# Attention round: the convolution's bias as a two-row product on TensorE, and statistics read from the PSUM bank

## The reference, cut to what matters

```
xp = einsum('mn,bnf->bmf', L_norm, x)
h  = xp @ Wc + bc                      # bc: a row of 128, the same for every node
h  = relu(layernorm(h) * g1 + be1)
x1 = h + x                             # q, k, v, attention, projection, two more layer norms follow
```

## Time and profile before

| | us |
|---|---|
| median of 3 runs | 1043.13 |
| lowest and highest | 1039.88, 1051.63 |
| the profiled execution's own time | 1042.99 |
| its span, first to last instruction | 1041.2 |
| VectorE busy in the span | 638.5 |
| TensorE busy in the span | 938.3 |
| TensorE's granted clock, mean | 0.946 |

### The profile page before, as it was taken

One profiled execution on the slowest core, in us unless ns is written; L12 is line 12 of the kernel. 1 busy time (PEld: TensorE's weight loads), 2 busy tenths in 40 slices (PEclk: granted clock), 3 DMA queues, 4 the chain that ended last, 5 costly groups with the idle time before them and its releaser, 6 DMA issues. The chain is left out here.

```text
span 1041.2 us, 21243 instructions
## 1 busy us (share of the span) xinstructions
PE 938.3 (90%) x7030; PEld 750.0 (72%) x7030; DVE 638.5 (61%) x2077; ACT 519.5 (50%) x1127; POOL 323.8 (31%) x405
## 2 busy tenths in 40 slices
PE   5998899999999999895999999999899999879771
PEld 4556799999999999875777767767676776647451
DVE  4743233333333335344788878878788888746998
ACT  2232322322332222212888877878787887855430
POOL 0000111111111112122335544545454553236665
PEclk8887999999999999898999998999999999989995
DMA  3000000000000000004544444544343444300111
GB/s 89 1 1 10 11 11 10 10 10 10 10 10 10 20 10 11 1 1 122 123 123 123 122 122 121 121 117 115 98 116 93 117 116 120 83 1 21 41 50 50
DMA packets 47199, 61.19 MB, mean 59 GB/s; under 512 B 4377, under 2 KB 22050, under 8 KB 47138
## 3 DMA queue, kind: packets, MB, share of 16 engines
q1 hardware_dynamic: 47138, 60.51, 22.7%
HBM read 39.53 MB, written 20.97 MB: 58 GB/s over the span
## 5 line engine op out<-in xcount | busy, mean ns | idle before, releaser
L1534 ACT ACTIVATE prob<-prob,low 128x512 f32<-128x512 f32 x256 | 184.1, 719 | 63.3 <-DVE low L1584 61.4
L1584 DVE CUSTOM_DVE_ANT_0 prob<-bank,mask 128x512 f32<-128x512 f32 x256 | 172.5, 685 | 41.5 <-PE bank L1413 24.7
L1426 PE MATMUL bank<-ident,prob 128*128 128x128 f32 x1024 | 164.7, 284 | 11.1 <-ACT probT L1523 11.0
L1426 PEld LDWEIGHTS bank<-ident,prob 128*128 128x128 f32 x1024 | 115.9, 143 | 58.4 <-issue 34.0
L1413 PE MATMUL bank<-k_stack,q_stack 128*128 128x512 f32 x256 | 125.4, 491 | 16.5 <-DVE low L1584 11.6
L1523 ACT ACTIVATE probT<-bank 128x512 f32<-128x512 f32 x176 | 102.5, 582 | 3.0 <-PE bank L1426 1.1
L1059 DVE TENSOR_TENSOR T_lo<-bank,T_hi 128x512 fp32r<-128x512 f32 x48 | 33.0, 688 | 112.0 <-ACT T_hi L897 112.0
L897 ACT ACTIVATE T_hi<-bank 128x512 fp32r<-128x512 f32 x48 | 28.4, 592 | 134.6 <-PE bank L807 91.6
L595 POOL TENSOR_SCALAR var_eps<-mv 128x4 f32<-128x4 f32 x16 | 3.6, 226 | 295.5 <-DVE mv L1012 295.5
L903 ACT ACTIVATE Sq<-bank,trace_inv 128x512 fp32r<-128x512 f32 x64 | 43.9, 686 | 92.3 <-PE bank L730 92.3
L1446 PE MATMUL bank<-probT,v 128*32 128x128 f32 x2048 | 83.0, 281 | 3.1 <-ACT probT L1523 1.1
(11 more groups left out here) (232 smaller groups left out, 1943.7 us busy)
## 6 DMA issues: line engine op xcount, KB each, us to landing
k_stack<-bounce_q SPq DMA_DIRECT2D x64, 256.0 KB, 5.0
q_stack<-bounce_k SPq DMA_DIRECT2D x64, 256.0 KB, 7.3
bounce_q<-k_parts SPq DMA_DIRECT2D x16, 512.0 KB, 2.8
bounce_k<-q_parts SPq DMA_DIRECT2D x16, 512.0 KB, 3.1
x_in<-in_x_dram SPq DMA_DIRECT2D x16, 256.0 KB, 2.8
out_dram<-result SPq DMA_DIRECT2D x16, 256.0 KB, 2.2
A<-in_adj_dram SPq DMA_DIRECT2D x4, 256.0 KB, 3.2
W1s<-in_L_gnn_W_dram SPq DMA_DIRECT2D x1, 128.0 KB, 2.4
```

The source lines that it names most:

```text
L1426: last = pe.transpose(psum[2 + u % 2][:, mt * P:(mt + 1) * P], prob[u % RING][:, mt * P:(mt + 1) * P], ident[:, :])
L1534: act.activation(prob[u % RING][:, :], prob[u % RING][:, :], ACT.Exp, bias=low[:, u % TURNED:u % TURNED + 1], scale=-1.0, accum_out=row_su ...
L1584: dve.tensor_tensor_reduce(prob[u % RING][:, :], psum[u % 2][:, :], mask[:, u // HEADS, :], 1.0, 3e38, ALU.add, ALU.min, low[:, u % TURNED ...
```

## The change

TensorE now opens A_BANK with one product of two rows: ones_parts (2 x 128 of ones) by bc_parts (2 x 128, broadcast to 2 x 512), the bias split into a high and a low part in the rounded format. The four tiles by W_c are added onto it. z_out is gone from the attention rounds. VectorE's statistics read A_BANK, and stand in unit 13, not 12; standardising reads A_BANK too, and stays in unit 14. Five small instructions of VectorE (split_bc) make the two parts once, ahead of the first attention round. The tile z takes the place of v_0, and three waits guard the reuse of tiles between stages.

```
 def biased_conv_weights(pe, one, bank, b):
+    pe.wait_ge(one.bc_step, 5)
+    pe.wait_ge(one.conv_ready, b + 1)
+    pe.matmul(bank[:, :], one.ones_parts, one.bc_parts.unsqueeze(1).broadcast_to([2, NT, D]),
+              start=True, stop=False, skip_group_check=True)
+    for t in range(NT):
+        last = pe.matmul(bank[:, t * D:(t + 1) * D], one.convT[:, t * P:(t + 1) * P], one.Wcs[:, :],
+                         start=False, stop=True, skip_group_check=True)
+    last.then_inc(one.z_psum, 1)
...
+def split_bc(dve, one):
+
+    row = one.bc_all[0:2, BC, :]
+    dve.wait_ge(one.rows_copied, 3)
+    dve.tensor_scalar(one.ones_parts, one.ident[0:2, :], 0.0, 1.0, ALU.mult, ALU.add).then_inc(one.bc_step, 1)
+    dve.tensor_copy(one.bc_hi, row).then_inc(one.bc_step, 1)
+    dve.wait_ge(one.bc_step, 2)
+    dve.tensor_tensor(out=one.bc_rest[0], in0=row, in1=one.bc_hi.bitcast(F32),
+                      op=ALU.subtract).then_inc(one.bc_step, 1)
+    dve.wait_ge(one.bc_step, 3)
+    dve.tensor_scalar(one.bc_rest[1], one.bc_rest[0], one.ident[0:2, 1:2], None,
+                      ALU.mult).then_inc(one.bc_step, 1)
+    dve.wait_ge(one.bc_step, 4)
+    dve.scalar_tensor_tensor(out=one.bc_parts, in0=one.bc_hi.bitcast(F32),
+                             scalar=one.ident[0:2, 0:1], in1=one.bc_rest[1], op0=ALU.mult,
+                             op1=ALU.add).then_inc(one.bc_step, 1)
...
+def z_bank_moments(dve, one, bank, b):
+    dve.wait_ge(one.z_psum, b + 1)
+    moments(dve, b, lambda t: bank[:, t * D:(t + 1) * D], one.b_stats, one.b_stats_ready, one.b_mv, one.b_mv_ready,
+            one.z_std_ready, b, one.dve_waited)
...
+def z_bank_standard(dve, one, bank, b):
+    dve.wait_ge(one.b_pool, 2 * b + 2)
+    at_least(dve, one.z_gain_ready, b)
+    for t in range(NT):
+        last = dve.tensor_scalar(one.z_std[:, t, :], bank[:, t * D:(t + 1) * D], one.b_mv[:, t, 0:1],
+                                 one.b_rstd[:, t:t + 1], ALU.subtract, ALU.mult)
+    last.then_inc(one.z_std_ready, 1)
...
-AT_CONV, AT_CONV_OUT, AT_Z, AT_Z_OUT, AT_Z_MOMENTS, AT_Z_STD = 6, 9, 10, 11, 12, 14
+AT_CONV, AT_CONV_OUT, AT_Z, AT_Z_MOMENTS, AT_Z_STD = 6, 9, 10, 13, 14
...
                         if u == AT_Z and within(r, 0, BATCH - 2):
-                            conv_weights(pe, one, A_BANK, r + 1)
+                            biased_conv_weights(pe, one, A_BANK, r + 1)
...
-                        if u == AT_Z_OUT and within(r, 0, BATCH - 2):
-                            z_out(dve, one, A_BANK, r + 1)
...
                         if u == AT_Z_MOMENTS and within(r, 0, BATCH - 2):
-                            z_moments(dve, one, r + 1)
+                            z_bank_moments(dve, one, A_BANK, r + 1)
...
                         if u == AT_Z_STD and within(r, 0, BATCH - 2):
-                            z_standard(dve, one, r + 1)
+                            z_bank_standard(dve, one, A_BANK, r + 1)
...
+                split_bc(dve, one)
                 rounds(dve, round_, 4, BATCH - 2, BATCH + 3, first=1)
```

More of the change, by code:

```diff
@@ L138, in two_layers @@
         one.convT = tensor(whole, "convT", [P, N])
-        one.z, one.z_std, one.z_gain, one.z_norm = (
-            tensor(whole, n, [P, NT, D]) for n in ("z", "z_std", "z_gain", "z_norm"))
+        one.row_parts = tensor(whole, "row_parts", [2, NT, D], F32R)
+        one.z = one.v[0]
+        one.z_std, one.z_gain, one.z_norm = (tensor(whole, n, [P, NT, D]) for n in ("z_std", "z_gain", "z_norm"))
         one.bounce = [[nc.dram_tensor(f"bounce_{n}{i}", (2, P, N), F32, kind="Internal").ap() for i in range(2)]
@@ L238, in conv_weights, with biased_conv_weights @@
     last.then_inc(one.z_psum, 1)
+def biased_conv_weights(pe, one, bank, b):
+    pe.wait_ge(one.bc_step, 5)
[32 more added lines that the diff above has]
+    last.then_inc(one.z_std_ready, 1)
 def z_out(dve, one, bank, b):
@@ L935, in round_ @@
                     if last_rounds == 2:
+                        act.wait_ge(one.z_std_ready, 2)
                         v_out(act, one, psum[4], 0, 0)
@@ L1215 @@
 AT_V, AT_V_OUT = 14, 14
-AT_CONV, AT_CONV_OUT, AT_Z, AT_Z_OUT, AT_Z_MOMENTS, AT_Z_STD = 6, 9, 10, 11, 12, 14
+AT_CONV, AT_CONV_OUT, AT_Z, AT_Z_MOMENTS, AT_Z_STD = 6, 9, 10, 11, 13
 AT_Y_MOMENTS, AT_H = 9, (11, 12, 13, 15)
@@ L1239, in layer1 @@
     Wos, W1s, W2s, b1s = one.Wos, one.W1s, one.W2s, one.b1s
-    x2_now = (one.z, one.z_std)
+    x2_now = (one.x1[0], one.z_std)
     x2T = (one.convT, one.x1T)
@@ L1301, in layer1 @@
         z2_std = sb("z2_std", [P, NT, D])
+        one.ones_parts, one.bc_parts = one.row_parts[:, 0, :], one.row_parts[:, 1, :]
+        one.bc_step = sem("bc_step")
         one.x1[1], one.v[1] = sb("x1_1", [P, NT, D]), sb("v_1", [P, NT, D])
@@ L1318, in layer1 @@
         h_parts = tuple(sb(f"h_{part}", [P, NT, D], F32R) for part in ("hi", "lo"))
+        one.bc_hi, one.bc_rest = z2[0:2, 0, :].bitcast(F32R), (z2_gain[0:2, 0, :], z2_std[0:2, 0, :])
         L_hi_ready, L_lo_ready, h_hi_ready, h_lo_ready = (
@@ L1561, in _ @@
                 act.wait_ge(x2_ready, 3)
+                act.wait_ge(one.x1T_psum, BATCH - 1)
+                act.wait_ge(one.x1_bo_ready, BATCH - 1)
                 fetch(act, 0, 0)
```

## The result

The changed kernel takes 1054.08 us (median of 20, 1048.65 to 1058.79) beside 1041.24 before (20 runs, 1036.88 to 1051.63). The ratio is 1.0111, with a 95% interval of 1.0086 to 1.0136. I had forecast 1071: slower was right, by 13 us and not by 28.

What follows compares the result with a forecast made beforehand. TensorE was taken to bound units 7 to 12 of a round, VectorE the rest to mask(6). 14 x 1.86 = 26.0 plus 1.8 for split_bc gives 27.8 us over 1043.13: forecast 1071 us, range 1047 to 1085.

Steps and rivals of the forecast that it cites:

- the pause in the jump rounds: In the four rounds where the loop jumps back, 2.9 us extra (29.29 against 26.40); the forecast kept it.
- the walk: Unit-by-unit reading of one plain attention round from unit 6; it had mask(15) and the residual 1.86 us later.
- What bounds the kernel: TensorE from unit 7 to 12, VectorE from there to mask(6).: The attention round's cycle: each engine bounds one half, within a plain round of 26.40 us.
- "The statistics moved behind mask(13): this is the part that counts.": VectorE, units 13 to 14: statistics done at 706.17, not 704.37, so z_std waits 0.39 us for its root.
- "add_bo follows the second residual and moves with the product": GpSimd's queue in an attention round: add_bo comes 0.23 us later.
- "In jump rounds VectorE itself comes last out of the jump, so a later arrival is a later start.": Rounds where the loop jumps back: they lengthen like the others, so 1.86 us is paid 14 times, 26.0.
- rival (c): Slower, but the 2.9 us extra where the loop jumps back takes up the shift: 20.4 us more, 1063; chance 0.12.
- "z_out removed ... Worth 0.": VectorE, unit 11: 14 x 0.61 = 8.5 us leave the queue where it waits for scores(12) anyway; worth 0.
- The two-row product, 0.23.: TensorE, unit 10: one matmul of 512 columns costs 0.23 us a round, bounds 0.2 and 0.5.
- z_std from the bank, 0.28 for four.: VectorE's four standardising instructions reading PSUM instead of SBUF: 0.28 us more a round, bounds 0 and 0.35.
- Statistics from the bank, 0.: VectorE's four statistics instructions reading PSUM: 0 to 0.3 us more a round, taken as 0.
- split_bc, 1.8.: VectorE, once, ahead of the first mask: five dependent small instructions cost 1.8 us, bounds 1.0 and 2.2.

Runs made afterwards that it cites:

- experiment 8: Changed kernel with GpSimd's z_root ahead of add_bo and without the two-row product (bias bc left out): 1019.72 us, ratio 0.9779 to the kernel before.
- experiment 2: Changed kernel with z_root ahead of add_bo in GpSimd's order, nothing else: 1028.82 us, ratio 0.9903 to the kernel before.
- experiment 1: Changed kernel with its statistics in unit 13 and standardising in unit 14, in place of 11 and 13: 1070.07 us, ratio 1.0265 to the kernel before.
- experiment 10: Changed kernel with 6 idle semaphore increments on VectorE ahead of the attention rounds: 1071.54 us, ratio 1.0276 to the kernel before.
- experiment 9: Kernel before with 12 idle semaphore increments on VectorE ahead of the attention rounds: 1027.29 us, ratio 0.9852 to the kernel before.
- experiment 11: Kernel before with 6 idle semaphore increments on VectorE ahead of the attention rounds, a control: 1041.3 us, ratio 0.9995 to the kernel before.

## Why the prediction was right or wrong

The direction was right, the size was not, and the mechanism was that of another kernel. Two steps failed: where the statistics stand and what their root waits for, and what becomes of the pause in the jump rounds. That a plain round grew by 2.0 where the walk had 1.86 is luck, since the wait in it is another one. The number missed by the second step: the forecast kept all four pauses, and they went, some 14 us. Point by point.

*What bounds the kernel: TensorE from unit 7 to 12, VectorE from there to mask(6).* It held. The product in TensorE's half cost all of its 0.62 (experiment 8), a wait in VectorE's half all of its 1.7 (experiment 2).

*"The statistics moved behind mask(13): this is the part that counts."* This is the first step that failed. They were moved ahead of mask(12), by my misreading of the diff. For its own kernel the step was sound (0.38 of wait for 0.39, experiment 1). For the real one the late party is not the root's own 1.61 us but add_bo ahead of it in GpSimd's order. I had listed that "add_bo follows the second residual and moves with the product", and didn't ask whom it holds up. I had no rival for it.

*"In jump rounds VectorE itself comes last out of the jump, so a later arrival is a later start."* Wrong, and the second step that failed: the forecast put nothing for the place of the code. The pause vanished, and not by cover, as rival (c) had it: the same late VectorE with six more instructions ahead has it in full (experiment 10). It was a matter of where the code lies. Worth in the kernel before: 1041.3 - 1027.3 = 14 us.

*"z_out removed ... Worth 0."* It fits the placement I had, where the plain round came out at 28.65 to 28.75 with nothing for z_out. In the real one the statistics move into the time that z_out left, and it counts: without the product and with the root first the rounds are 26.03, against 26.40 with the old code. Only this difference of 0.37 is measured; that it is z_out's 0.61 less the bank's dearer read of 0.29 is argued, and leaves 0.05.

*The two-row product, 0.23.* Mis-sized: 0.62 to 0.64, above my upper bound of 0.5.

*z_std from the bank, 0.28 for four.* 1.37 against 1.11, so 0.26. *Statistics from the bank, 0.* 0.89 against 0.86. By the table of costs in the Trainium skill's "VectorE: DVE Perf Modes" I had estimated 0.5 for the eight; they cost 0.29 more here, and the measurement decides.

*split_bc, 1.8.* Mis-sized too: five instructions from 487.11 to the first mask at 488.38, 1.3, all in the queue in front of that mask.

The sum by rounds, at equal code placement: 0.63 (product) + 1.73 (root behind add_bo) + 0.26 (bank) + 0.03 - 0.61 (z_out) = 2.04; measured 28.4 - 26.4 = 2.0. Of two kernels without the pause, changed and experiment 9, the first mask to the last took 437.3 and 411.6 us. That is 25.7 apart, not quite thirteen rounds' worth, since the first interval isn't longer; with split_bc's 1.3 it makes 27.0, and the medians lie 1054.1 - 1027.3 = 26.8 apart. Before with its pause (experiment 11) stands 1041.3 - 1027.3 = 14 above the lower of these: 27 - 14 = 13 is what was measured. Without the accident of placement the change costs 27 us. With the root first it costs little, but still brings nothing: rounds of 26.67 against 26.40, 1028.8 us against 1027.3.

## What to carry to other kernels

When a step is moved, list for each engine what stands ahead of its successors in their queues, and ask what that waits for: here GpSimd's harmless add_bo came to stand between a statistic and its root. Test a change of a few instructions near a hand-written loop with a few idle instructions in front: two kernels are compared fairly only when neither loop pays the pause, or both do. And read the constants of a diff twice.

## What the runs showed of the hardware that was not expected

A loop's place in the instruction stream is worth 14 us of 1041: a jump round is about 2.9 us longer, more where the granted clock falls behind it (31.14 at 0.89), if 270 instructions lie across four blocks of 128 rather than three. The block of 128 and the shift are worked out from the fourteen kernels and the size of the packets. What exactly is kept and what is dropped in such a turn no run here shows.

A product of two rows by 512 columns in the rounded format takes 0.43 us to the next start where 128-row products of the same width follow each other in 0.23; whether the broadcast operand, the change of format or the short rows do it was not tried.

Standardising out of SBUF beside a GpSimd operation on SBUF took 1.93 us in place of 1.11, and one instruction of the four had the whole of it; out of PSUM the four took 1.37 beside 0.6 us of the same operation and 1.36 to 1.37 without it. Why about every second round of experiment 1 is longer and has a lower clock stays open.
